# Two of every four adjacency masks made on GpSimd instead of VectorE in a graph-attention and expert-FFN kernel

## What is computed

```
q = (ht @ Wq + bq).reshape(T, H, HD) / sqrt(HD)        # T = S = 2048, H = 8 heads, HD = 32
k = (hs @ Wk + bk).reshape(S, H, HD)
v = (hs @ Wv + bv).reshape(S, H, HD)
logits = einsum('thd,shd->hts', q, k)
logits = where(edge_mask != 0, logits, -1e30)          # edge_mask: int32 2048 x 2048, the same for all heads
probs  = softmax(logits, axis=-1)
ctx    = einsum('hts,shd->thd', probs, v)
...                                                    # Wo, layer norm, FFN, residual
...                                                    # 8 experts, two for each token
```

## Time and profile before

| what | value |
|---|---|
| median of 3 runs | 1123.71 us |
| lowest and highest | 1119.06 and 1127.06 us |
| the profiled execution: its span, first to last instruction | 1127.1 us |
| busy: PE, DVE, ACT, POOL | 967.3, 675.2, 748.1, 577.1 us |
| attention, roughly | 86 to 700 us of the span |

### The profile page before, as it was taken

One profiled execution on the slowest core, in us unless ns is written; L12 is line 12 of the kernel. 1 busy time (PEld: TensorE's weight loads), 2 busy tenths in 40 slices (PEclk: granted clock), 3 DMA queues, 4 the chain that ended last, 5 costly groups with the idle time before them and its releaser, 6 DMA issues. The chain is left out here.

```text
span 1127.1 us, 21116 instructions
## 1 busy us (share of the span) xinstructions
PE 967.3 (86%) x6828; PEld 587.3 (52%) x6828; DVE 675.2 (60%) x1963; ACT 748.1 (66%) x949; POOL 577.1 (51%) x474
## 2 busy tenths in 40 slices
PE   2962489989999999998999998798940999999994
PEld 1631144434444444443444454456740898998983
DVE  6833677777777877777777753654643343443431
ACT  4521389979999999998999984654320645555551
POOL 6503469886777777776755874200354122323231
PEclk9985589989999999999999998999965999999998
DMA  6498564574436635457256325850542123323233
GB/s 196 104 282 271 183 188 148 197 261 139 171 120 232 244 112 181 158 194 248 97 184 213 117 92 205 313 207 25 201 166 75 45 45 59 53 46 59 36 46 93
DMA packets 74012, 169.27 MB, mean 150 GB/s; under 512 B 13490, under 2 KB 43058, under 8 KB 68210
## 3 DMA queue, kind: packets, MB, share of 16 engines
q1 hardware_dynamic: 49634, 98.41, 26.4%
q0 software_dynamic: 20416, 68.32, 20.3%
q10 hardware_dynamic: 3856, 1.19, 0.5%
HBM read 121.65 MB, written 62.36 MB: 163 GB/s over the span
## 5 line engine op out<-in xcount | busy, mean ns | idle before, releaser
L1023 DVE CUSTOM_DVE_ANT_0 masked<-ps,maskA 128x512 f32<-128x512 f32 x512 | 347.2, 689 | 120.5 <-PE ps L1452 117.6
L1452 PE MATMUL ps<-ks,qs 96*128 96x512 f32 x512 | 261.4, 550 | 53.6 <-DMA qs<-q_low 27.8
L1339 ACT ACTIVATE masked<-masked,negmax 128x2048 f32<-128x2048 f32 x128 | 256.3, 2003 | 69.1 <-DVE negmax L1029 68.5
L1400 ACT ACTIVATE weights<-ps 128x1024 f32<-128x1024 f32 x256 | 253.8, 1014 | 37.6 <-PE ps L1475 35.1
L1473 PE MATMUL ps<-qs,ks 98*128 98x512 f32 x512 | 230.5, 509 | 3.7 <-DMA qs<-shift_lo 3.7
L1475 PE MATMUL ps<-maskB,identb 128*128 128x512 bf16 x512 | 202.6, 396 | 0.0
L1452 PEld LDWEIGHTS ps<-ks,qs 96*128 96x128 f32 x512 | 102.3, 200 | 141.1 <-DVE piecemax L1023 95.2
L1722 POOL DMA_INDIRECT sum_rows<-y,ids x42 | 65.2, 1552 | 179.8 <-DVE y L1760 160.2
L1487 PE MATMUL ps<-weights,v_all 128*32 128x256 f32 x2048 | 138.0, 387 | 0.9 <-ACT weights L1400 0.9
L1742 DVE TENSOR_TENSOR gT<-ffn_w,gT 128x2048 f16<-128x2048 f32 (+1 forms) x23 | 48.5, 2107 | 133.0 <-ACT gT L1799 133.0
L842 POOL TENSOR_SCALAR wch<-wch 128x1024 f32<-128x1024 f32 x36 | 100.3, 2786 | 36.3 <-DMA wch<-in_L_gnn_W 32.2
(11 more groups left out here) (188 smaller groups left out, 1124.2 us busy)
## 6 DMA issues: line engine op xcount, KB each, us to landing
expert_rows<-pad_rows POOLq DMA_DIRECT2D x73, 272.0 KB, 6.0
split_weights<-whl POOLq DMA_DIRECT2D x36, 512.0 KB, 3.2
adjA<-in_adj SPq DMA_DIRECT2D x16, 1024.0 KB, 8.1
adjB<-in_adjT SPq DMA_DIRECT2D x32, 512.0 KB, 6.7
wall<-split_weights SPq DMA_DIRECT2D x16, 1024.0 KB, 15.1
wch<-in_w1T POOLq DMA_DIRECT2D x16, 512.0 KB, 6.2
wch<-in_w2T POOLq DMA_DIRECT2D x16, 512.0 KB, 6.2
xr<-expert_rows SPq DMA_DIRECT2D x19, 272.0 KB, 2.9
```

The costliest lines, as they stand in the source:

```text
L1023: dve.tensor_tensor_reduce(masked[:, a % 2, k * 512:(k + 1) * 512], ps[:, u % 2, :], maskA[:, a, k * 512:(k + 1) * 512], 1.0, NO_EDGE, ALU ...
L1339: act.activation(masked[:, a % 2, :], masked[:, a % 2, :], ACT.Exp, bias=negmax[:, h % 2, a:a + 1], accum_out=rowsum[:, h % 4, a:a + 1]).t ...
L1400: act.activation(weights[:, j % 4, :, :], ps[:, 2 + 2 * (j % 2):4 + 2 * (j % 2), :], ACT.Exp).then_inc(weights_ready, 1)
L1452: pe.matmul(ps[:, u % 2, :], qs[0:KR, h % 4, a * P:(a + 1) * P], ks[0:KR, h, k * 512:(k + 1) * 512], start=True, stop=True)\
```

## The change

In the three boundaries the masks of tiles 1 and 3 are made by POOL instead of DVE, with the same operation on the same data. Tiles 0 and 2 stay on DVE, where they were. The four masks of block 0, at the start, stay on DVE too. The semaphore `maskA_ready` becomes two, one for even tiles and one for odd ones, so that each counts one engine's work. DVE now waits, at the first piece of each tile in a block's first head, for that tile's mask. A semaphore is saved elsewhere (`pad_step` goes into `pool_step`), and POOL's scaling of the weights is written with two factors, 64 and 1.

```
-                    sp.wait_ge(pad_step, 2)
+                    sp.wait_ge(pool_step, 4)
...
-        maskA_ready = sem("maskA_ready")
+        maskA_ready = [sem(f"maskA_ready{i}") for i in range(2)]
...
                 for a in range(2, TPB):
-                    sp.wait_ge(maskA_ready, a - 1)
+                    sp.wait_ge(maskA_ready[a % 2], a // 2)
                     load_adjA(a, a)
...
                     if h in (H - 4, H - 3) and b + 1 < NB:
                         for a in range(2 * (h - H + 4), 2 * (h - H + 5)):
-                            sp.wait_ge(maskA_ready, TPB * (b + 1) + a - 1)
+                            sp.wait_ge(maskA_ready[a % 2], 2 * (b + 1) + a // 2)
                             load_adjA((b + 1) * TPB + a, a)
...
                     wait_apart(pool, wch_in, 16 * i + 16)
-                    pool.tensor_scalar(wch[:, :], wch[:, :], WSCALE, None, ALU.mult).then_inc(wch_scaled, 1)
+                    pool.tensor_scalar(wch[:, :], wch[:, :], WSCALE, 1.0, ALU.mult, ALU.mult).then_inc(wch_scaled, 1)
...
+                def mask_a(b, a):
+
+                    pool.wait_ge(maxima_read, UNITS * H * b - UNITS + UPT * (a + 1))
+                    pool.wait_ge(adjA_in[a % 2], 16 * (b * (TPB // 2) + a // 2 + 1))
+                    pool.tensor_scalar(maskA[:, a, :], adjA[:, a % 2, :], 0.0, NO_EDGE, ALU.is_equal, ALU.mult)\
+                        .then_inc(maskA_ready[a % 2], 1)
...
                 for n in range(N):
                     b, h = divmod(n, H)
                     e = 2 * b + h // 4
+                    if b + 1 < NB and h == H - 2:
+                        mask_a(b + 1, 3)
                     if b + 1 < NB:
                         mask_b(b + 1, h)
                     if n == N - 1:
                         row_factors(0, 1)
                     if n:
                         scale_context(n - 1, (n - 1) % H)
+                    if b + 1 < NB and h == H - 3:
+                        mask_a(b + 1, 1)
                     split(n + 4)
...
                             at_least(dve, rowsum_ready, TPB * n + a - 1)
+                            if n % H == 0:
+                                dve.wait_ge(maskA_ready[a % 2], 2 * (n // H) + a // 2 + 1)
...
-                        if h == H - 3 and b + 1 < NB and u % UPT == UPT - 1:
+                        if h == H - 3 and b + 1 < NB and u in (UPT - 1, 3 * UPT - 1):
 
                             mask_a(b + 1, u // UPT)
-                    if h == H - 2 and b + 1 < NB:
-                        dve.wait_ge(maskA_ready, TPB * (b + 2))
                     maxima(n + 2, n % 2, beside)
```

More of the change, by code:

```diff
@@ L156, in graph_attention_and_experts @@
         ones_made = sem("ones_made")
-        pad_step = sem("pad_step")
         pad_out = sem("pad_out")
@@ L276, in _ @@
                     scale_rows(hh, range(NT), hn_ready, hn_scaled)
-                    pool.memset(pad[:, :, :], 0.0).then_inc(pad_step, 1)
-                    pool.wait_ge(pad_step, 1)
+                    pool.memset(pad[:, :, :], 0.0).then_inc(pool_step, 1)
+                    pool.wait_ge(pool_step, 3)
                     pool.iota(pad[:, :, D + E], pattern=[[P, 2]], base=T, channel_multiplier=1,
-                              allow_small_or_imprecise_dtypes=True).then_inc(pad_step, 1)
+                              allow_small_or_imprecise_dtypes=True).then_inc(pool_step, 1)
                 @block.vector
@@ L759, in _ @@
                         load_constants()
-                        sp.wait_ge(maskA_ready, TPB * NB)
+                        for i in range(2):
+                            sp.wait_ge(maskA_ready[i], 2 * NB)
                         load_h(0)
@@ L981, in mask_a @@
                     dve.tensor_scalar(maskA[:, a, :], adjA[:, a % 2, :], 0.0, NO_EDGE, ALU.is_equal, ALU.mult)\
-                        .then_inc(maskA_ready, 1)
+                        .then_inc(maskA_ready[a % 2], 1)
                 def mask_b(b, h):
@@ L1052, in mask_next_tile @@
                         mask_a(0, a)
-                        dve.wait_ge(maskA_ready, a + 1)
                 steps = [0]
@@ L1209, in _ @@
                 mask_a(0, 0)
-                dve.wait_ge(maskA_ready, 1)
                 maxima(0, 0, mask_next_tile)
```

## The result

| kernel | median | lowest and highest | runs |
|---|---|---|---|
| before | 1121.38 us | 1118.83 to 1127.06 | 4 |
| changed | 1137.85 us | 1136.57 to 1141.28 | 4 |

The changed kernel is slower: the ratio is 1.0143, with a 95% interval of 1.0111 to 1.0176. The forecast was 1137. The profiled execution of the changed kernel spans 1135.4 us and took 1137.18 us, so an execution is about 1.8 us longer than its span. The profiled execution of before must therefore have taken about 1129 us, more than any of the four runs in the table; that its span equals the slowest of the three times shown is chance.

What follows compares the result with a forecast made beforehand. PE was taken to pace attention. Each boundary: 0.33 (tile 0's mask) + 7.3 (shift) + 1.8 (clock) = 9.4 us; three, 28.3 against 14.3, add 14.0 to 1127.1, giving 1141.1, less 3.4 for the median: 1137. Range 1116 to 1150.

Steps and rivals of the forecast that it cites:

- The direction and the cause: At each boundary SP's tile 3 load waits for POOL's mask, delaying the shift some 7 us; 14.0 us slower in all.
- One sign named ahead: At each boundary PE's longest idle of the step ends by the DMA of `shift_lo`, 6 to 8 us.
- The mask on POOL: At a boundary, a POOL mask of 2048 columns takes 7.3 us undisturbed, six times DVE's.
- The meeting of DVE and POOL: At a boundary, DVE's tile 2 mask runs unslowed inside POOL's tile 1 mask, which is stretched to 8.3 us.
- PE's wait: At the second boundary PE wants the shift at 386.6, but it lands at 393.9: a wait of 7.3 us.
- the rival: At boundaries DVE waits for POOL, unstretched at 7.3 us; PE waits 6.3, a boundary costs 8.4, total 1134.7; chance 0.20.
- The clock: After PE's long wait at each boundary the granted clock drops, losing 1.8 us.
- The sum: Three boundaries at 9.4 us cost 28.3 us against 14.3 before: 14.0 us more.
- The scaling: POOL's two-factor scaling of the weights was taken at 2.79 us, as with one factor, and costs nothing.
- Tile 3 on POOL: POOL's mask of tile 3 ends at 406.1, DVE reads it at 409.3: 3 us to spare, no cost.

Runs made afterwards that it cites:

- shift first: The changed kernel with the store of the shift ahead of the load of adjacency tile 3 in SP's list; 1130.49 us, 1.0077 of before.
- held but not queued: The changed kernel where SP still waits for POOL's mask of tile 1, then stores the shift, then loads tile 3; 1132.01 us, 1.0093 of before.
- second profile of before: The kernel before, unchanged, profiled again; one run, 1130.20 us, its three boundaries costing 11.6 us.
- third profile: The kernel before, unchanged, profiled a third time; one run, 1125.48 us, its three boundaries costing 11.5 us.
- one factor: The changed kernel with POOL's scaling in one factor, as before; 1137.51 us, 1.0153 of before.
- tile 2 late: The changed kernel with DVE's mask of tile 2 made beside u = 14 instead of u = 11; 1140.32 us, 1.0144 of before.
- Both edits: The changed kernel with the shift stored ahead of tile 3's load and DVE's tile 2 mask beside u = 14; 1119.14 us, again 1119.35 us.
- the two results: The kernel before with only the two-factor scaling, run twice; 1118.79 us (0.9962 of before) and 1119.03 us (0.9978).

## Why the prediction was right

**The direction and the cause.** SP's load of tile 3, waiting for POOL's mask of tile 1 with the shift behind it, did what the prediction said: at the second boundary the load left when that mask ended, the shift 0.7 us later, and PE's wait ended by `shift_lo` when the load had landed. One sign named ahead came only in part: no single idle time of PE was 6 to 8 us, and the longest ended by the shift only at the first boundary (3.18 us against 3.13 for DVE); at the other two it ended by DVE (3.03 and 3.01 against 2.48 and 2.42). The experiments with the shift first, and held but not queued, show that these are causes and not only neighbours in time.

**The mask on POOL** was put at 7.3 us; it took 7.1.

**The meeting of DVE and POOL** was the step that failed. The prediction chose that DVE's mask of tile 2 would run through and POOL's be stretched to 8.3 us, by the one row where that had happened; it gave the other outcome a chance of 0.20. The other came, at all three boundaries: DVE's mask took about 4 us and POOL's was not stretched. The Trainium skill's rule ("SBUF — State Buffer", Who interferes with whom), that with VectorE in a two-port mode the one that starts first keeps the shared ports for its whole instruction, agrees with these three meetings.

The trace of before had more meetings than the prediction read. Against its choice stood the longest mask of all, tile 1 of the first boundary, which stood still behind POOL's scaling and caused the 1.85 us of the earlier trace rows:

```profile
240.70 2.77 POOL L842 TENSOR_SCALAR wch<-wch 128x1024 f32<-128x1024 f32 x1
```

```profile
241.91 2.64 DVE L981 TENSOR_SCALAR maskA<-adjA 128x2048 bf16<-128x2048 int32 x1
```

And the POOL mask of 389.67, which the prediction called undisturbed, had a mask of DVE inside it, from 1.09 us after its start, and neither was slowed (3.66 us, against 3.65 without one):

```profile
390.76 1.22 DVE L981 TENSOR_SCALAR maskA<-adjA 128x2048 bf16<-128x2048 int32 x1
```

The meeting of 511.65, the row that the choice rested on, went the other way in the second profile of before: DVE's mask stood still and POOL's kept its time.

```profile
507.36 3.65 POOL L861 TENSOR_SCALAR maskB<-adjB 128x1024 bf16<-128x1024 int32 x1
```

```profile
510.14 1.96 DVE L981 TENSOR_SCALAR maskA<-adjA 128x2048 bf16<-128x2048 int32 x1
```

In the first and the third profile DVE's mask began 2.58 and 2.59 us after POOL's and ran through; in the second, and in the kernel with one factor, it began 2.78 and 2.74 us after it and stood still. What decides such a meeting is not shown; the rule alone explains neither the 2.58 nor the 1.09.

**PE's wait.** Forecast 7.3 us for the shift, or 6.3 in the rival; measured 6.3, 5.5 and 5.4, split into a first part that ends by DVE and a second by the shift. The rival had said that DVE's standing still hides under the wait for the shift; tile 2 late shows that it does.

**The clock.** Forecast 1.8 us a boundary. What is left of 9.1, 7.6 and 8.9 us after the waits (0.3 + 6.3, 0.3 + 5.5, 0.3 + 5.4) is 2.5, 1.8 and 3.2. It is a remainder, not measured by itself. Two things tie it to the clock. Both edits, which take away the long waits, take it away too. And at the second boundary of before, where no wait is longer than 0.6 us, the clock reads 1.00 (columns as in the earlier trace rows) and the 2.16 us are PE's waits alone, 2.17 together:

```profile
382.00:390.00 8.00, 6.67 (x48) 2.86 (x37) 7.31 (x21) 6.35 (x8) 7.07 (x8) 1.00 0.60 207
```

**The sum.** Forecast 28.3 us for the boundaries of the changed kernel, 25.3 in the rival, measured 25.6. Less before's 14.3 that is 11.3 us, less the 11.5 of the later profiles 14.1; the medians differ by 16.5. The 1137 was met with a difference too large by 2.7 us for the boundaries, put on a median that lay 2.3 us above the later one. So 2 to 5 us of the difference between the medians are not found at the boundaries; whether they are chance or another stage was not settled. They are no more than single executions differ elsewhere: the span less what the boundaries cost is 1112.8, 1116.8 and 1112.2 us in the three profiles of before and 1109.8 in that of the changed kernel, and 1106.0 and 1114.5 in those with the shift first and held but not queued. That the forecast lies within 1 us of the median is luck: a base too high by 2.3 us and a difference too low by 2.5 (14.0 against 16.5) cancelled.

**The scaling** was put at 2.79 us between 1.07 and 3.66, and came out just under the lower end. That it costs nothing held in the changed kernel (one factor); in the kernel before the two results are 0.9962 and 0.9978, the second with an interval that reaches 1, and its boundaries cost 7.4 and 9.0 us instead of 11.5 to 14.3, since DVE's masks stand still less. The prediction did not see that.

**Tile 3 on POOL** cost nothing in the changed kernel, as said: no wait of PE or DVE for it shows at any boundary. At the second the mask ended at 403.22 and DVE came to it at 408.77, 5.5 us later (forecast 3.2). That room came from the waits ahead of it; with both edits they are gone, and DVE waits 1.5 us for the mask.

## What to carry to other kernels

When work goes from one engine to another, look at every queue that waits for its signal and at what stands behind that wait: here a load that nobody was in a hurry for held a 2 KB store that PE needed at once. Put the urgent DMA ahead of the big one in a list, even when both are ready. Place an instruction of DVE that stands still behind POOL where POOL's long ones are not: three pieces later was enough, once the shift no longer waited. And when a wait has been taken away, see again what was in time only because of it: here POOL's second mask.

## What the runs showed of the hardware

- A scaling of 128 x 1024 float32 in place on POOL takes 2.77 us with one factor and 1.04 us with two, the second being 1.
- DVE's mask, 1.22 us alone, took 3.93 us when it began 4.2 us into a 7.08 us instruction of POOL; the instruction of POOL behind it then took 1.90 us instead of 1.04. Begun 2.58 us into a 1024-column mask of POOL it ran in 1.22 us, and POOL's took 4.69 us instead of 3.65; begun 2.78 us into one it took 1.96 us and POOL's 3.65; begun 1.09 us into one it slowed nothing.
- A store of two rows behind a 1 MB load in SP's queue let its reader start 4.0 us after its issue; ahead of the load it was in use 1.7 us after its issue.
